# Moving the end work of the first batch's four chunks into groups four to six of attention

## What is computed

```python
Q, K, V = (proj(Wq), proj(Wk), proj(Wv))
O = _flash_attention(Q, K, V, BLOCK, scale)        # causal, 16 heads of 16
x = _layernorm(x + O @ Wo.T)
lhs_scale = max(|x| of a token) / 127              # and so for the weights' columns
acc = round(x / lhs_scale) @ round(rhs / rhs_scale)
x = _layernorm(x + acc * lhs_scale * rhs_scale)
```

## Time and profile before

| what | us |
|---|---|
| median of 3 runs (1010.09 to 1015.05) | 1012.61 |
| the profiled execution | 1015.52 |
| its span, first to last instruction | 1013.8 |
| group 5 | 99.8 |
| group 6 | 107.4 |
| last group | 123.2 |
| behind the last exponential | 41.1 |

### The profile page before, as it was taken

The page is one execution under the profiler, slowest core; times in us unless marked ns, Lnnn a source line. Parts: engine busy times, 40 slices in busy tenths (PEclk is TensorE's granted clock), DMA queues, the critical chain, the costliest instruction groups (busy, mean ns, idle before and its releaser), DMA issues.

```text
span 1013.8 us, 34409 instructions
## 1 busy us (share of the span) xinstructions
PE 946.2 (93%) x14884; PEld 474.4 (47%) x14884; DVE 821.1 (81%) x1083; ACT 710.9 (70%) x1470; POOL 264.3 (26%) x431
## 2 busy tenths in 40 slices
PE   8899999999999999999999999999999999999862
PEld 5555545544554454445444644454444444434331
DVE  5488878887888788878887888788878886799797
ACT  3434348787878877887888788878877687777630
POOL 4443442102210221022102210211022104456534
PEclk9999989999999999999999999999999999999985
DMA  5556530001210121022002200220022050434501
GB/s 176 163 180 183 153 116 10 8 9 45 69 36 9 49 66 34 9 58 64 28 8 66 64 24 6 72 65 19 8 72 68 11 132 14 131 84 115 147 32 52
DMA packets 71836, 67.29 MB, mean 66 GB/s; under 512 B 15113, under 2 KB 65609, under 8 KB 71685
## 3 DMA queue, kind: packets, MB, share of 16 engines
q1 hardware_dynamic: 71684, 65.10, 22.9%
HBM read 43.25 MB, written 21.35 MB: 64 GB/s over the span
## 4 chain that ended last, share of the span: by engine, by line
PE 71%; DVE 14%; ACT 7%; DMA 3%; issue 2%; POOL 1%; SPq 1%; POOLq 0%; DVEq 0%; ACTq 0%
PE ps_acc L723 20%; PE ps_max L679 19%; PE ps_score L679 18%; DVE block_max L970 6%; ACT PR L922 6%; PE ps_score L602 4%; PE ps_score L609 2%; PE ps_max L677 2%; PE ps_max L697 2%; DVE stats L1084 1%; DMA end_slots<-heads_out 1%; ACT accS L910 1%; DMA V<-heads_out 1%; PE ps_max L797 1%; DVE end_slots L1094 1%
## 5 line engine op out<-in xcount | busy, mean ns | idle before, releaser
L970 DVE TENSOR_REDUCE block_max<-ps_max 128x2 f32<-128x1024 f32 (+3 forms) x640 | 653.8, 1061 | 141.8 <-PE ps_max L679 68.6
L922 ACT ACTIVATE PR<-ps_score 128x512 f32<-128x512 f32 (+3 forms) x1280 | 620.3, 539 | 169.0 <-PE ps_score L679 150.0
L679 PE MATMUL ps_score<-QS,KS 99*32 99x512 bf16 (+3 forms) x5120 | 418.0, 351 | 22.7 <-ACT PR L922 19.2
L679 PE MATMUL ps_max<-KS,QS 96*32 96x512 bf16 (+3 forms) x4544 | 329.2, 350 | 7.4 <-DVE block_max L970 5.3
L723 PE MATMUL ps_acc<-PR,VG 128*32 128x512 f32 (+3 forms) x2560 | 299.1, 534 | 0.0
L679 PEld LDWEIGHTS ps_score<-QS,KS 99*32 99x32 bf16 x5120 | 150.3, 96 | 216.9 <-ACT PR L922 119.3
L679 PEld LDWEIGHTS ps_max<-KS,QS 96*32 96x32 bf16 x4544 | 126.3, 97 | 141.8 <-DVE block_max L970 59.8
L1192 POOL TENSOR_SCALAR_AFFINE_SELECT PR<-PR 128x512 f32<-128x512 f32 x128 | 81.6, 638 | 285.8 <-ACT PR L922 285.8
L697 PE MATMUL ps_max<-mask_q,ident_b 128*32 128x64 bf16 (+3 forms) x1808 | 96.1, 200 | 0.0
L723 PEld LDWEIGHTS ps_acc<-PR,VG 128*32 128x32 f32 x2560 | 79.3, 110 | 35.4 <-issue 3.5
L1200 POOL CAST max_parts<-neg_max 16x128 bf16<-16x128 f32 (+1 forms) x30 | 8.7, 289 | 224.9 <-ACT neg_max L905 223.5
(11 more groups left out here) (126 smaller groups left out, 525.0 us busy)
## 6 DMA issues: line engine op xcount, KB each, us to landing
QS<-qparts SPq DMA_DIRECT2D x192, 64.0 KB, 2.4
KS<-kparts SPq DMA_DIRECT2D x192, 64.0 KB, 2.4
qparts<-end_slots SPq DMA_DIRECT2D x16, 384.0 KB, 3.8
kparts<-end_slots SPq DMA_DIRECT2D x16, 384.0 KB, 3.1
PR<-in_L_attn_x SPq DMA_DIRECT2D x8, 512.0 KB, 4.4
heads_out<-accS SPq DMA_DIRECT2D x124, 32.0 KB
end_slots<-in_L_attn_x SPq DMA_DIRECT2D x4, 512.0 KB, 9.4
out_y<-end_slots SPq DMA_DIRECT2D x8, 256.0 KB, 2.1
```

The source lines that it names most:

```text
L679: m = pe.matmul(bank[t * QW:t * QW + QW, 0:w], stack[:, t * QW:t * QW + QW], moving, start=True, stop=stop)
L922: act.activation(PR[:, k % 4, j, 0:w], ps_score[:, score_slot(pos), 0:w], ACT.Exp, scale=SCALE).then_inc(s_exp, 1)
L970: dve.tensor_reduce(block_max[:, h * PAIR:h * PAIR + PAIR, i, b], ps_max[:, slot_at:slot_at + PAIR, 0:w], AX.X, ALU.max).then_inc(s_reduce ...
```

## The change

The eight halves of the first batch leave the last group. Chunk m starts at step 170 + 28 m (`SOON_START`), its second half 14 steps later; only the two projections of the second half stand 2 steps behind those of the first. So they lie in steps 170 to 285. Their projection, turn and product no longer use `ps_max` but are further uses of the three score banks, in one numbering of all uses (`bank_order`), and ScalarE empties the bank each time: it copies the projection into `hid`, the turned integers, and the product times the token's scale. The weights' scale is multiplied in by GpSimd (two operations of 256 columns a half) in place of VectorE's L1145. The residual then reads SBUF and not PSUM. The second batch keeps its way through `ps_max`, at steps 294, 297, 302, 305, 314, 316, 321 and 322. Projection and product are now four column tiles of 32 for all halves (`tiled`), but for those of the very last chunk's projection. The slots are four; chunks 2 and 3 and later 6 and 7 reuse those of chunks 0 and 1. `quota` gets the group's number and counts the end work (`PE_END`, `DVE_END`), so the items of groups 4, 5 and 6 are spread anew; those of groups 0 to 3 stay. The loop code with `behind`, `turned` and `wait_apart` goes: a bank waits for the third use back throughout, and 29 semaphore marks of TensorE are dropped.

```diff
+    ENDS = B * CHUNKS
+    HALF = CH // 2
+    TPH = HALF // P
+    SOON = 4
+    SOON_HALVES = 2 * SOON
+    SLOT = [0, 1, 0, 1, 2, 3, 0, 1]
+    SLOTS = 4
+    ALL = GROUPS * NS
+    FIRST_END, LAST_GROUP = 4 * NS, (GROUPS - 1) * NS
+    SOON_START = [FIRST_END + 10 + 28 * m for m in range(SOON)]
+    CHUNK_START = SOON_START + [LAST_GROUP + k for k in (14, 22, 34, 35)]
+    PROJECT_START = [at + 2 * s for at in SOON_START for s in range(2)]
+    HALF_START = [at + 14 * s for at in SOON_START for s in range(2)] + \
+        [LAST_GROUP + k for k in (14, 17, 22, 25, 34, 36)] + [ALL + 1, ALL + 2]
+    CHUNK_DUE = dict(sums_in=-8, sums_back=-6, load=-4, outputs=-2)
+    SOON_DUE = dict(residual=5, rstd1=6, norm1=7, quantise=8, to_int=9, turn=10, product=12, residual2=13, moments2=14,
+                    rstd2=15, norm2=16, store=17)
+    DUE = dict(project0=0, project1=0, residual=1, rstd1=2, norm1=3, quantise=3, to_int=5, turn=6, take=6, product=7,
+               scale=8, residual2=9, moments2=10, rstd2=11, norm2=12, store=13)
+    DONE_AT = max(HALF_START) + max(DUE.values())
...
-    LAG, BATCH = 2, 1
+    LAG = 2
     LOAD, READ, READ_FROM = 256, 2.5, 340
...
+    PE_END = dict(project0=2048, project1=2048, product=1024, turn=800)
+    DVE_END = dict(residual=4600, norm1=2000, quantise=6000, moments2=2900, norm2=2000)
+
+    def quota(stream, g):
 
...
+        work = lambda k, parts: sum(cost * len(soon_due(NS * g + k, part)) for part, cost in parts.items())
...
-                if k % BATCH == BATCH - 1:
-                    at += sum(HG * (CH - skip(*STEPS[k - back])) for back in range(LAG, LAG + BATCH))
+                at += work(k, PE_END) + HG * (CH - skip(*STEPS[k - LAG]))
+                done = max(done, at if work(k, DVE_END) else 0) + work(k, DVE_END)
...
-    SLOTS = 6
-    HALF_START = [3 + 5 * e // 2 for e in range(2 * ENDS - 2)] + [NS + 1, NS + 2]
-    CHUNK_START = HALF_START[:-2:2] + [HALF_START[-4] + 1]
-    EARLY_LOADS = 2
-    DUE = dict(sums_in=-7, sums_back=-6, load=-5, outputs=-3, project0=0, project1=0, residual=1, rstd1=2, norm1=3,
-               to_int=5, turn=6, take=6, product=7, scale=8, residual2=9, moments2=10, rstd2=11, norm2=12, store=13)
...
+                for part in ("product", "turn", "project0", "project1"):
+                    order += [(part, e) for e in soon_due(NS * g + k, part)]
+                order += [("maxima", g + on, c) for at, on, c in TURNS[g] if at == k]
         return {use: n for n, use in enumerate(order)}
...
-    def behind(pos):
-
-        return min(3, next(d for d in range(1, 9) if (pos - d >= 0 and score_slot(pos - d) == score_slot(pos))
-                           or (pos - d < 0 and score_slot(UNITS + pos - d) == score_slot(pos))))
...
-        room = [(end_words[:, :], 6), (V_words, 8), (QS_words[:, 0:HG * T // 2], 4)]
+        room = [(end_words[:, :], 6), (V_words, 6)]
...
-                        if kind == "full" and k == FULL_LOADS:
-                            for m in range(CHUNKS):
-                                sums_back(m)
-                            for m in range(EARLY_LOADS):
-                                load(m)
+                        if k in STACKS_AT and 0 < g < GROUPS - 1:
+                            load_stacks(nq, np_, STACKS_AT.index(k))
+                        end_parts(NS * g + k)
...
+                            if j % 2:
+                                project(NS * g + k, j // 2)
+                        soon_parts(NS * g + k)
+                        end_parts(NS * g + k)
                         if k >= LAG:
-                            values(g, k - LAG, kind)
-                        elif not first:
...
+                def soon_parts(k):
+
+                    for e in soon_due(k, "product"):
+                        m, s = divmod(e, 2)
+                        use = USE["product", e]
+                        pe.wait_ge(s_exp, max(USE["turn", e] + 1, use - BANKS + 1))
+                        for t in range(TPH):
+                            at = s * HALF + t * P
+                            for h in range(HALVES):
+                                y = tiled(ps_score[:, bank_of(use), t * D:t * D + D], hqT(m)[:, h, at:at + P], ffn_q[:, h, :],
+                                          h)
+                        y.then_inc(s_st, 1)
...
+                    for t in range(TPH):
+                        for e in soon_due(k, f"project{t}"):
+                            m, s = divmod(e, 2)
+                            use, at = USE[f"project{t}", e], s * HALF + t * P
+                            pe.wait_ge(e_on, HALVES * (m + 1))
+                            pe.wait_ge(s_exp, use - BANKS + 1)
+                            for h in range(HALVES):
+                                y = tiled(ps_score[:, bank_of(use), 0:D], o_in(m)[:, h, at:at + P], wT[:, 3, h, :], h)
+                            y.then_inc(s_st, 1)
+
+                def tiled(out, stack, moving, h):
+
+                    for r in range(0, P, QW):
+                        y = pe.matmul(out[r:r + QW], stack[:, r:r + QW], moving, start=h == 0, stop=h == HALVES - 1)
+                    return y
...
-                            y = pe.matmul(ps_max[:, s, t * D:t * D + D], o_in(m)[:, h, at:at + P],
-                                          wT[:, 3, h, :], start=h == 0, stop=h == HALVES - 1)
+                            y = tiled(ps_max[:, s, t * D:t * D + D], o_in(m)[:, h, at:at + P], wT[:, 3, h, :], h)
...
+                            y = act.activation(work(m)[:, at, :], ps_score[:, bank_of(use), t * D:t * D + D], ACT.Identity,
+                                               scale=lscale[:, SLOT[m], at:at + 1])
+                        y.then_inc(s_exp, 1)
...
+                            act.copy(half_of(hid(m), s)[:, t, :], ps_score[:, bank_of(use), 0:D]).then_inc(s_exp, 1)
...
-                        if kind == "full" and place == len(STREAM[kind]) // 2:
-                            for m in range(CHUNKS):
-                                invert_sums(m)
...
+                def group(g):
+                    n = 0
+                    for k in range(NS):
+                        while n < QUOTA[g][k][-1]:
+                            on, m = STREAM[KIND[g]][n]
+                            item(g + on, m, maxima_use(g + on - 1, ITEMS[m][0] // TPC) + 1 if g + on else 0)
+                            n += 1
+                        end_parts(NS * g + k)
...
+                            dve.wait_ge(s_exp, USE["project1", e] + 1)
+                            y = half_of(hid(m), s)
+                        else:
+                            dve.wait_ge(e_y, TPH * (late(e) + 1))
+                            y = ps_max[:, s, :].rearrange("p (t d) -> p t d", d=D)
+                        dve.tensor_tensor(half_of(work(m), s), y, half_of(work(m), s), ALU.add).then_inc(e_res, 1)
...
+                            pool.wait_ge(s_exp, USE["product", e] + 1)
+                            for t in range(s * TPH, s * TPH + TPH):
+                                pool.tensor_tensor(work(m)[:, t, :], work(m)[:, t, :], ffn_scale[:, :], ALU.mult)\
+                                    .then_inc(e_wide, 1)
+                            pool.wait_ge(e_wide, TPH * (e + 1))
```

438 lines of the change are left out of this document (197 added, 241 removed).

## The result

The changed kernel takes **1051.09 us** (median of 4 runs, 1044.12 to 1052.29) against 1012.81 for the kernel before in the same comparison: ratio 1.0365, 95% interval 1.0312 to 1.0418. It is slower by 38 us; the forecast was 1011, in a range of 999 to 1022. The forecast was wrong.

What follows compares the result with a forecast made beforehand. The prediction took TensorE as the bound, with VectorE and ScalarE a sixth to a fifth free. Groups 4 to 6 +26.3, last group -24.0, tail -3.2, numbering and marks -0.3 gave -1.2 on 1012.6: 1011 us, range 999 to 1022.

Steps and rivals of the forecast that it cites:

- TensorE's 20.3 us: Groups 4 to 6: 16 projections, 8 turns and 7 products add 20.3 us to TensorE, with nothing hiding them.
- VectorE's waits, 9.5 us: Groups 4 to 6: late maxima behind VectorE's end work stop TensorE for 1.5, 3 and 5 us, 9.5 in all.
- The share that was to warn of trouble, 90 to 99%: VectorE's needed time as a share of TensorE's in groups 4, 5 and 6: 90, 95 and 99%.
- "Zero" for ScalarE and the banks: ScalarE's copies for the extra score-bank uses fit its free time: zero cost, high bound 5 us.
- "Zero, high bound 2 us a chunk" for GpSimd, SyncE and the loads: First-batch loads land in time and GpSimd has room for its added work: zero cost, at most 2 us a chunk.
- rival (c): Late loads: GpSimd waits for landings with masks behind it, 2 us at each of four chunks, 1019; chance 0.07.
- The last group, -24.0: Without the first batch's end work the last group takes 99.2 us in place of 123.2, 24.0 shorter.
- rival (e): Last group: the load for chunks 6 and 7 waits for its own heads, 20 off, 1015; no separate chance.
- The tail, -3.2: Behind the last accumulator copy: chunk 5 starts six steps earlier and is done by then, 3.2 us shorter.
- The inversions, -3.5: Group 6: inverting row sums one per chunk, not in one burst, saves 3.5 us.
- (b): VectorE becomes the bound in groups 4 to 6, 342.6 us in all, and the kernel gets slower, 1020; chance 0.20.
- (d): VectorE's SBUF operations lose time to a port shared with GpSimd, 22 us more for VectorE, 1026; chance 0.05.

Runs made afterwards that it cites:

- e12: The kernel before with the four row sums of the first batch inverted one at a time, not in a row: 1011.74 us, ratio 0.9976.
- e13: e10 without the first batch's projections, turns and products on TensorE, ScalarE's copies of them and the 31 bank uses: 999.49 us, ratio 0.9859.
- e10: e9 with TensorE's projections and products, ScalarE's copies of them and GpSimd's second residual also on 8 of 256 columns: 1008.35 us, ratio 0.9951.
- e9: e6 with the items placed where the kernel before has them: 1025.11 us, ratio 1.0120.
- e1: The changed kernel with the first batch's sums, inverses, outputs and tokens loaded or stored earlier: 1038.35 us, ratio 1.0255.
- e6: e1 with VectorE's first-batch end operations on 8 of 256 columns, their number, order and waits kept: 1031.93 us, ratio 1.0184.
- e14: e10 with VectorE's quantisation of a half as one operation, not six, and a normalising as one, not two: 1001.91 us, ratio 0.9899.
- e7: e1 with ScalarE's first-batch copies out of the banks and GpSimd's second-residual operations on 8 of 256 columns: 1033.86 us, ratio 1.0219.
- e2: The changed kernel with chunks 4, 5 and 6 started later in the last group, at steps 18, 25 and 36: 1057.56 us, ratio 1.0450.
- e4: The kernel before with only the late projections and products in four column tiles of 32: 1011.57 us, ratio 0.9992.

## Why the prediction was wrong

The lengths of groups 4 to 6, taken apart step by step, with TensorE's busy and idle time in them:

| kernel | groups 4 to 6 | busy | idle | what is added | us |
|---|---|---|---|---|---|
| before | 307.0 | 297.8 | 9.2 | | |
| e12 | 304.7 | 296.5 | 8.2 | the inversions apart | -2.3 |
| e13 | 311.7 | 299.0 | 12.7 | VectorE's, GpSimd's and ScalarE's end operations, small | 7.0 |
| e10 | 321.9 | 307.0 | 14.9 | TensorE's projections and products, small, the turns, 31 bank uses | 10.2 |
| e9 | 335.5 | 321.4 | 14.1 | full sizes on TensorE, ScalarE, GpSimd | 13.6 |
| e1 | 350.0 | 326.8 | 23.2 | full sizes on VectorE, and the items' places round them | 14.5 |
| changed | 362.3 | 331.5 | 30.8 | the loads late | 12.3 |

Busy and idle time are read from the views by stretch, before, e12 and e9 here, the others from their rows above:

```profile
542.50:849.50 307.00, 297.77 (x5668) 147.38 (x5660) 257.56 (x268) 241.24 (x505) 51.63 (x109) 0.99 0.19 50
```

```profile
544.70:849.40 304.70, 296.49 (x5667) 146.15 (x5660) 257.24 (x268) 241.39 (x504) 51.41 (x109) 1.00 0.19 51
```

```profile
543.50:879.00 335.50, 321.37 (x6067) 157.40 (x6060) 276.30 (x412) 260.20 (x550) 93.54 (x168) 1.00 0.23 61
```

The 55.3 of them with -19.5 and -0.2 behind and 0.9 ahead are the 36.6 us between the spans, within 0.1. Of the 14.5, 3.4 is lower clock, and of the 12.3, nearly 5.

- **TensorE's 20.3 us** stands: in e9 the 16 projections make 13.8 us, the 8 turns 2.6 and the 7 products 3.1, 19.5 together, each from its start to that of what follows. The tiled projection takes 0.86 us as predicted, from its start to that of the values (timeline of TensorE, changed kernel, group 5):

```profile
737.97 1.03 PE L766 MATMUL ps_score<-wT,end_slots 128*32 128x256 f32 x16
738.83 1.03 PE L695 MATMUL ps_acc<-PR,VG 128*32 128x512 f32 x8
```

- **VectorE's waits, 9.5 us,** is the first step that failed. It was sized from one burst with a discount for gaps in the order. Measured: 14.5 for sizes and places, 3.4 of it clock, and 7.0 for the small operations (GpSimd's and ScalarE's among them), so about 18 without the clock. TensorE's idle time rises by 9.1 and 4.5 us in these two steps of the table. What was left out is that an operation costs its fixed part and its wait however small it is (e6, e14); and a burst can also reach the scores through ScalarE's queue. The share that was to warn of trouble, 90 to 99%, never came (79 to 86%, and 84 to 87% in e1). VectorE's part shows elsewhere: in the chain of work that ended last its maxima hold 9.2% of the three groups in the kernel before, 28.5% in e13 and 25.1% in e1.
- **"Zero" for ScalarE and the banks,** with a bound of 5, held: 2.2 us of idle time at 31 bank uses, 4.1 at most (e13), and the sizes of ScalarE's copies are free (e7).
- **"Zero, high bound 2 us a chunk" for GpSimd, SyncE and the loads** is the other step that failed, 12.3 us for four chunks, nearly 5 of it the lower clock behind the waits. The step behind it was rival (c)'s "28 steps leave the queues empty". The distance between chunks says nothing of what stands just ahead: chunk 0's sums are due in step 2 of group 4, behind step 1's stack loads. Landing times were read, queue places weren't, though the order had them.
- **The last group, -24.0,** came as -19.5. The plain steps (2.18 us) and the projection steps that wait for nothing (3.46 and 3.11) are near the forecast. The term that failed is the waiting for landings, put at 1 us: the steps in which chunks 4 and 6 start take 9.53 and 6.96 us, 9.5 more than two projection steps, with TensorE waiting 4.9 and 3.3 us for GpSimd. The other terms came 4 us lower than forecast. This is rival (e), 20 in place of 24. Starting later doesn't help (e2).
- **The tail, -3.2,** failed: 40.9. VectorE's busy time in it fell by 2.4 us (32.8 to 30.4) and the stretch by 0.2, so the work for chunk 5 seems to have lain beside the chain that ends last, not on it; no run tests this.
- **The inversions, -3.5:** the mechanism was right and the size near, 2.4 (e12).
- **The rivals.** (b), the kernel gets slower by VectorE, gave the groups 342.6 us, near e1's 350.0 (346.6 without the clock). It had the right engine, but it reasoned from a VectorE at 90%, which none of the traces shows (84 to 87%), so the nearness of the number is in part luck. (c) had the right place and two thirds of the price (8 of 12.3), though the larger part came by VectorE's wait for the sums and not by GpSimd's. (d), a lock of VectorE against GpSimd: the rounding takes 427/428/737 ns (min/median/max of its 12 in `end_slots`) in the changed kernel, and the residual, now with two inputs in SBUF, 0.68 us in the median and 0.78 at most where it was 0.68. VectorE is busy for 301.6 us in the three groups, where the forecast had 307.4 without any such loss. (By the prediction's own count 7.35 halves lie there, not 7.7.) The rule of the Trainium skill, page "SBUF — State Buffer", section "SBUF: two separate sides", may act at single operations here; as a cost of 22 us it didn't appear.

The error was one of kind. Each engine's added work was weighed against that engine's free time. The free time was there (VectorE 14% and more, ScalarE more), and the terms for work were right. Of the 55.3 us TensorE is busy for 33.7, of which 6.6 is lower clock, and idle for 21.6, where the forecast had 6.0 for all waits and inversions together. What was missed is idle time of TensorE, behind VectorE and behind late loads, and the clock that fell with it.

Open: how e1's 14.5 us splits between VectorE's sizes and the uneven places (e6 and e9 say 8.1 and 6.4, without the clock 6.4 and 4.7), which of the small operations make e13's 7.0, and what the way through ScalarE's queue costs. No run has the last group's loads issued earlier in their queue.

## What to carry to other kernels

Work moved into a stage whose bound engine is full costs its own time there (here 19.5 us, for 20.3 forecast), and what comes with it on the engine that feeds the bound one costs waits as well, though that engine has time free: here some 18 us for VectorE's 43 us of added busy time. Count the operations and where they stand, not only the free time; made small, they kept a good part of their price. For every DMA that is given a new place, read which DMAs its queue issues in the ten microseconds ahead of it. Before paying for a move, cut the same work where it stands (as e4): if the stage doesn't get shorter, the engine that you relieve isn't its bound.
